# A graph attention layer on one core: three target buffers, scatters behind the queries, strips added four groups back

## What is computed

```python
w_ij = silu(edge_feats @ rad_W1 + rad_b1) @ rad_W2 + rad_b2
w_ij = w_ij + (silu(chi_scalar @ sph_W1 + sph_b1) @ sph_W2 + sph_b2)
q_i = (node_feats @ Wq)[receivers]                 # 8 heads of 16
k_j, v_j = (node_feats @ Wk)[senders], (node_feats @ Wv)[senders]
alpha = (q_i * w_ij * k_j).sum(axis=-1) / sqrt(16) * cutoffs[:, None]
out = segment_sum(alpha[..., None] * v_j, receivers) / 16
return layernorm(node_feats + out)
```

## Time and profile before

| | |
|---|---|
| median of 3 runs | 1971.99 us (1971.89 to 1974.09) |
| the profiled execution | 1972.41 us, of which the program's span 1970.7 us |
| busy share of the span | TensorE matmul 88%, weight load 64%, VectorE 80%, GpSimd 76%, ScalarE 29% |
| granted TensorE clock | 0.937 of 2.4 GHz, mean over the span |
| DMA | 339.02 MB, mean 172 GB/s |

### The profile page before, as it was taken

How to read it: one execution, slowest core, us unless ns; L and a number is a source line. 1 busy time by engine, 2 the same in 40 slices (tenths; PEclk the granted TensorE clock), 3 DMA queues, 4 the chain that set the end, 5 groups by cost and what they waited for, 6 DMA issues and landing times.

```text
span 1970.7 us, 56844 instructions
## 1 busy us (share of the span) xinstructions
PE 1729.7 (88%) x14511; PEld 1261.0 (64%) x14511; DVE 1569.1 (80%) x4324; ACT 580.7 (29%) x1030; POOL 1488.5 (76%) x1569
## 2 busy tenths in 40 slices
PE   8789889898989988888988898989888888898887
PEld 7566666666666656666666666666666666666665
DVE  5578888787877878877978877878778788788787
ACT  5322232222322322322332222232222222222223
POOL 7777777777777777777777777777777777777777
PEclk9899899998988999998999998998899899889898
DMA  9866656666656556556556555656656565656554
GB/s 338 259 172 172 165 163 174 163 169 168 168 161 171 165 166 171 163 165 173 164 164 174 161 167 164 173 164 173 164 165 167 160 175 162 165 163 166 172 156 116
DMA packets 191076, 339.02 MB, mean 172 GB/s; under 512 B 82989, under 2 KB 101022, under 8 KB 190750
## 3 DMA queue, kind: packets, MB, share of 16 engines
q0 software_dynamic: 74240, 202.21, 36.5%
q1 hardware_dynamic: 107440, 126.14, 22.2%
q10 hardware_dynamic: 9070, 7.02, 1.6%
HBM read 320.25 MB, written 14.95 MB: 170 GB/s over the span
## 4 chain that ended last, share of the span: by engine, by line
PE 22%; DMA 21%; SPq 20%; POOL 18%; issue 13%; DVE 5%; DVEq 1%; ACT 0%; ACTq 0%
POOL kvt L655 18%; DMA dbt<-dst 14%; SPq L582 13%; PE bank L693 10%; DMA kvt<-kvtab,srcS 4%; PE bank L670 3%; SPq L576 3%; SPq L591 2%; PE bank L708 2%; DMA out<-partn 2%; PE bank L695 2%; PE bank L732 2%; DVE t L979 1%; PE bank L301 1%; PE bank L683 1%
## 5 line engine op out<-in xcount | busy, mean ns | idle before, releaser
L655 POOL DMA_INDIRECT kvt<-kvtab,srcS x1528 | 1450.9, 950 | 466.3 <-issue 456.5
L770 ACT ACTIVATE hs<-bank,B 128x512 f32<-128x512 f32 x806 | 510.5, 685 | 1350.3 <-issue 804.6
L693 PE MATMUL bank<-W2r,hs 128*128 128x128 f32 x3224 | 499.5, 302 | 8.3 <-ACT hs L770 8.3
L693 PEld LDWEIGHTS bank<-W2r,hs 128*128 128x128 f32 x3224 | 424.2, 205 | 86.6 <-issue 75.3
L693 PE MATMUL bank<-W2s,hs 128*128 128x128 f32 x3224 | 456.7, 288 | 0.0
L966 DVE TENSOR_TENSOR t<-bank,kvt 128x512 f32<-128x512 f32 (+1 forms) x396 | 265.4, 670 | 207.9 <-PE bank L695 131.9
L693 PEld LDWEIGHTS bank<-W2s,hs 128*128 128x128 f32 x3224 | 424.8, 205 | 0.0
L708 PE MATMUL bank<-msg,oh 128*32 128x128 f32 x3216 | 179.0, 294 | 164.0 <-DVE accT L913 160.6
L708 PEld LDWEIGHTS bank<-msg,oh 128*32 128x32 f32 x3216 | 70.6, 110 | 355.7 <-issue 300.4
L981 DVE TENSOR_REDUCE bank<-t 128x32 f32<-128x512 f32 x403 | 280.1, 695 | 13.9
L979 DVE TENSOR_TENSOR t<-bank,t 128x512 f32<-128x512 f32 x403 | 274.2, 680 | 4.2 <-PE bank L683 3.2
(11 more groups left out here) (106 smaller groups left out, 702.7 us busy)
## 6 DMA issues: line engine op xcount, KB each, us to landing
kvA<-kvtab ACTq DMA_DIRECT2D x3968, 1.0 KB
eft<-in_ef SPq DMA_DIRECT2D x102, 512.0 KB, 7.7
kvS<-kvtab SPq DMA_DIRECT2D x3200, 1.0 KB
dbt<-dst SPq DMA_DIRECT2D x102, 384.0 KB, 6.1
kvt<-kvtab,srcS POOLq DMA_INDIRECT x1528
qwt<-qtab SPq DMA_DIRECT2D x403, 24.0 KB
kvtab<-kvt SPq DMA_DIRECT2D x24, 256.0 KB, 7.9
qtab<-qx SPq DMA_DIRECT2D x12, 384.0 KB, 6.3
```

The source lines that it names most:

```text
L655: pool.indirect_dma_start(kvt[:, (g - HX) % KS, t, :], None, kvtab, bass.IndirectOffsetOnAxis(ap=srcS[:, g * TG + t:g * TG + t + 1], axis= ...
L693: pe.matmul(WB[g % 2][:, t * D:(t + 1) * D], hs[:, g % HS, j, t * 128:(t + 1) * 128], w2[:, :], start=(j == 0 and t == 0), stop=False, ski ...
L770: act.activation(hs[:, g % HS, j, :], HB[i % 4][:, :], ACT.Silu, bias=B1[:, j:j + 1]).then_inc(m_si, 1)
```

## The change

- Targets `dbt` get three buffers, and SyncE loads them at g % 4 == 0 instead of g % 4 == 2.
- The first product `t1` gets one buffer instead of two, the messages three instead of four. From group 400 on L999 waits for the scatter of g - 3; in earlier groups `collect(g - 3)` has waited for it.
- TensorE runs in each group: layer 2, the fold of g - 4, the queries, the scatter of g - 3, layer 1. Before, the scatter stood first and the fold was that of g - 3.
- VectorE adds the strips of g - 4 instead of g - 3 and copies those of g - 3 out instead of g - 2. Squares, refinements, scaling and stores of finished nodes come one group later.
- In the prologue the turned features and the remainders lie in two of the three buffers of `eft`, and SyncE waits for the projections of the first groups too.

```diff
-    KS, ES, DS, QS, HS, MS, OS, WS = 15, 3, 2, 6, 4, 4, 3, 6
+    KS, ES, DS, QS, HS, MS, OS, WS = 15, 3, 3, 6, 4, 3, 3, 6
...
-        t1 = sb("t1", [128, 2, TG, D], f32)
+        t1 = sb("t1", [128, TG, D], f32)
...
-            xgT = psb("xgT", [128, 2, G], f32)
+            xgT = eft[:, 2, :, :]
...
-            def qleft(t, b):
-                return t[:, b % 2, 0:min(4, NC - 4 * b), :]
+            qrest = eft[:, 1, :, :].rearrange("p k (a f) -> p k a f", f=D)
+
+            def qleft(b):
+                return qrest[:, b % 2, 0:min(4, NC - 4 * b), :]
...
+            dve.wait_ge(s_win, 4)
             for b in range(NQB + 1):
...
-            act.wait_ge(s_hp, 2 * HX)
+            for eng in (act, sp):
+                eng.wait_ge(s_hp, 2 * HX)
...
-                if b < NQP and (g == 0 or g % 4 == 2 and b >= 2):
+                if g % 4 == 0 and b < NQP:
                     if b >= DS:
                         sp.wait_ge(m_ot, 4 * (b - DS + 1))
...
             for g in range(NE):
-                if 3 <= g < NE - 2:
+                l2(g)
+                if g >= 4:
+                    fold_tiles(g - 4)
+                gq(g)
+                if g >= 3:
                     scat(g - 3)
-                l2(g)
-                if g >= NE - 2:
-                    scat(g - 3)
-                    gq(g)
-                if g >= 3:
-                    fold_tiles(g - 3)
-                if g < NE - 2:
-                    gq(g)
                 if g % 2 == 0 and g // 2 + 1 < NP:
                     l1(g // 2 + 1)
             scat(NE - 3)
+            fold_tiles(NE - 4)
             scat(NE - 2)
...
-                if 3 <= g < NE - 2:
-                    accumulate(g - 3)
+                if 4 <= g < NE - 2:
+                    accumulate(g - 4)
...
-                if 0 <= g - 2 < LC:
-                    collect(g - 2)
+                if 0 <= g - 3 < LC:
+                    collect(g - 3)
                 if g >= NE - 2:
-                    accumulate(g - 3)
+                    accumulate(g - 4)
...
                 dve.wait_ge(m_al, g + 1)
+                if g - MS >= LC:
+                    dve.wait_ge(m_sc, g - MS + 1)
...
+            accumulate(NE - 4)
             accumulate(NE - 3)
             accumulate(NE - 2)
```

More of the change, by code:

```diff
@@ L459, in gnn_program @@
                     act.wait_ge(s_r0, b)
-                    act.activation(qpart(b - 1, 1), qleft(t1, b - 1), ACT.Copy).then_inc(s_q2, 1)
+                    act.activation(qpart(b - 1, 1), qleft(b - 1), ACT.Copy).then_inc(s_q2, 1)
                 if b == NQB // 2:
@@ L475, in gnn_program @@
                         dve.wait_ge(s_q3, b - 1)
-                    dve.tensor_tensor(qleft(t1, b), qfull(b), qpart(b, 0), ALU.subtract).then_inc(s_r0, 1)
+                    dve.tensor_tensor(qleft(b), qfull(b), qpart(b, 0), ALU.subtract).then_inc(s_r0, 1)
                 if b >= 1:
                     dve.wait_ge(s_q2, b)
-                    dve.tensor_tensor(qpart(b - 1, 2), qleft(t1, b - 1), qpart(b - 1, 1),
+                    dve.tensor_tensor(qpart(b - 1, 2), qleft(b - 1), qpart(b - 1, 1),
                                       ALU.subtract).then_inc(s_q3, 1)
@@ L622, in gnn_program @@
                 sp_rows(g)
-                if g - 17 in use_n:
-                    store(use_n[g - 17])
+                if g - 18 in use_n:
+                    store(use_n[g - 18])
             q, b = max(range(0, NQP, ES)), max(range(0, NQP, DS))
@@ L629, in gnn_program @@
             destinations(0, m_db[0])
-            for g in range(NE, NE + 17):
-                if g - 17 in use_n:
-                    store(use_n[g - 17])
+            for g in range(NE, NE + 18):
+                if g - 18 in use_n:
+                    store(use_n[g - 18])
             sp.wait_ge(m_ef[0], features_landed(q) + 16)
@@ L813, in late_collect @@
                     act.activation(part[:, g % 2, :], strips(g)[:, 0:D], ACT.Copy).then_inc(m_part, 1)
-            for g in range(NE + 12):
+            for g in range(NE + 13):
                 if g < NE:
                     silu(g)
[L818 to L821, removed]
+                if g - 6 in use_n and use_n[g - 6] not in late:
+                    square(use_n[g - 6])
+                if g - 13 in use_n and use_n[g - 13] not in late:
+                    scale(use_n[g - 13])
                 if g < NE:
@@ L965, in gnn_program @@
                 for a, b, kv in kv_parts(g):
-                    m = dve.tensor_tensor(t1[:, s, a:b, :], tiles(WB[s][:, :])[:, a:b, :], kv[:, :, 0:D], ALU.mult)
+                    m = dve.tensor_tensor(t1[:, a:b, :], tiles(WB[s][:, :])[:, a:b, :], kv[:, :, 0:D], ALU.mult)
                 m.then_inc(m_t1, 1)
-                if 3 <= g < NE - 2:
-                    accumulate(g - 3)
+                if 4 <= g < NE - 2:
+                    accumulate(g - 4)
                 if g + 2 < NE:
                     window_T(g + 2)
-                if g - 5 in use_n:
-                    first_guess(use_n[g - 5])
+                if g - 6 in use_n:
+                    first_guess(use_n[g - 6])
                 for i in range(3):
-                    if g - 6 - i in use_n:
-                        refine(use_n[g - 6 - i], i)
+                    if g - 7 - i in use_n:
+                        refine(use_n[g - 7 - i], i)
                 dve.wait_ge(m_t1, g + 1)
                 dve.wait_ge(m_q, g + 1)
-                dve.tensor_tensor(t2[:, :, :], tiles(QB[:, :]), t1[:, s, :, :], ALU.mult).then_inc(m_t2, 1)
+                dve.tensor_tensor(t2[:, :, :], tiles(QB[:, :]), t1[:, :, :], ALU.mult).then_inc(m_t2, 1)
                 dve.wait_ge(m_t2, g + 1)
```

## The result

The changed kernel takes 1986.55 us (median of six runs, 1981.92 to 1988.46) against 1973.35 (six runs, 1971.89 to 1974.38) for the kernel before: a ratio of 1.0066 (95% interval 1.0056 to 1.0076; intervals stand in square brackets from here on), 13.2 us slower. The prediction was 1976.0, with a range up to 1982. The profiled execution is the quickest of the six, 1981.92 us, span 1980.2, mean granted clock 0.965 (before 0.937).

A forecast was written before the change was run, and what follows sets the result against it. GpSimd's gathers were taken to set the end, compute having 67 us in hand. Profiled 1972.4 + 0 + 1.3 + 2.7 = 1976.4, less 0.4 for the median: 1976.0 us, range 1973 to 1982.

The forecast's parts named there:

- The price of the path: Loop: product, add, scatter, layer 1, layer 2 now in series; some 0.27 us a group more, between 0 and 0.27.
- the cover: Loop: gathers allow compute 4.685 us a group; 0.09 a group, 37 us, stays in hand, so 0 at the end.
- the 0.19: Loop: VectorE's vanished waits for targets, up to 78.0 us over 403 groups, give back up to 0.19 us a group.
- predicted own pace of 4.59: Loop: compute's time a group without waits for gathers, 4.515 + 0.27 - 0.19 = 4.59 us.
- Step 1 of the tail: Last groups: group 400's rows used at 1951.5 (1951.1 to 1952.3), group 401's first product at 1956.4 (1956.0 to 1957.1).
- step 3: From group 402's first product to the last scatter's end: later adds, scatters and folds in series, +2.7 us (1.5 to 3.0).
- Step 2: Group 401 to 402: scatter 398 waits for a late add ahead of layer 2; 402's first product at 1961.65, +1.3 (0.9 to 2.0).
- the gathers' stream: GpSimd's gathers, untouched: 0 us, +-1; again 1.255 us apart, the last starting within 1 us of 1956.9.
- the 78.0 us of waits for targets worth 0: VectorE's 45 waits for targets go, but the gathers hide the gain: 0 at the end, otherwise up to 78 us.
- the prediction's rival: VectorE bounds the kernel, so removing its target waits takes up to 78.0 us off: 1894 us; chance 0.04.
- the first waits for gathers: Sign on VectorE: its waits for gathered rows begin well before 1200 us and sum to above 67 us.
- outruns the gathers: Loop rival: the new scatter path exceeds 4.685 us a group; 1998 us at 4.75, at most 2011; chance 0.12.

The follow-up runs named there:

- targets alone: Kernel before with only the target buffers and loads, first-product and message buffers and prologue changed, order as before: 1977.00 us, 1.0002 (0.9977 and 0.9978 on slow chips).
- the change again: The changed kernel unaltered, run a second time beside the kernel before for a second profile: 1986.51 us against 1972.85, ratio 1.0070.
- early adds alone: Changed kernel with the adds of the last two groups behind the first product, as in all other groups: 1983.30 us, 1.0031 to the kernel before.
- layer 1 ahead: Changed kernel with layer 1 put ahead of the scatter of g - 3: 1983.24 us, 1.0032 to the kernel before (1.0006 on a slow chip).
- both repairs: Changed kernel with layer 1 before the scatter and the last two groups' adds behind the first product: 1979.69 us, 1.0014 to the kernel before.

## Why the prediction was wrong

**The step that failed** is the one on the loop: "Its cover is the 4.685 that the gathers allow; 0.09 a group, 37 us, is left", costed at 0. The price of the path was right, the cover was not: before the tail's own part begins, group 401's first product is 3.8 us late in the first profile, and 6.0 in the second, counted from its last gather. Three sub-steps:

1. *The mean hid two phases.* From group 7 to 247 compute takes 4.651 us a group before (109.9 to 1226.1) and 4.669 after, though 0.27 was to be added and 0.19 given back; the targets alone take 4.65 too. Some other limit holds that phase, so the 0.19 had nothing to come from. From group 247 to 402, without the waits for gathers, it takes (734.3 - 67.2)/155 = 4.30 before, from 1226.1 to 1960.36, and (737.2 - 27.5)/155 = 4.58 after, from 1229.5 to 1966.73. **The difference is 0.28, the 0.27 of the prediction.** It goes with the order: counted alike, the change again takes 4.62 and the early adds alone 4.56, but the targets alone 4.34, layer 1 ahead 4.36 and both repairs 4.30. That 4.58 is also close to the predicted own pace of 4.59 is luck: the base was 0.21 too high for this phase, and the 0.19 given back never came; over the whole run the prediction's own count gives (1857.7 - 27.5)/395 = 4.63.
2. *What counts is not the margin of the mean but how fast a delay is made good.* By the mean the cover would have done: the gathers come at 4.84 us a group, so 4.58 makes the 22.4 us of group 247 good in some 86 groups of 155, and compute did catch up and wait for rows. But those waits lie ahead of the delays that count at the end. In two quiet stretches, picked from the traces, compute regains 0.89 us a group before (9.21 to 4.75 us late from group 375 to 380), 0.68 in the change (13.89 to 9.14 from 387 to 394). And delays are larger: at groups 369 and 385, each the first product behind a layer 1 with only three gathers, the kernels with layer 1 behind the scatter lose 1.1 to 4.1 us, the others 0.3 to 1.7 (table).
3. *The largest of these delays in the first profile starts at a wait for a gather.* The timeline of the changed kernel at group 384, and its windows (busy us of PE, PEld, DVE, ACT and POOL, granted clock, DMA share, GB/s):

```profile
1881.17 0.69 DVE L967 TENSOR_TENSOR t<-bank,kvt 128x512 f32<-128x512 f32 x1 [1.44 <-DMA kvt<-kvtab,srcS]
...
1882.14 0.66 PE L712 MATMUL bank<-msg,oh 128*32 128x128 f32 x8 [2.42 <-DVE accT L914]
...
1882.73 2.09 PE L674 MATMUL bank<-eft,W 32*128 32x512 f32 x8
...
1884.75 2.08 PE L697 MATMUL bank<-W2r,hs 128*128 128x128 f32 x8
...
1888.81 0.56 DVE L967 TENSOR_TENSOR t<-bank,kvt 128x384 f32<-128x384 f32 x1 [3.37 <-PE bank L699]
```

```profile
1884.00:1887.00 3.00, 3.00 (x14) 2.25 (x11) 1.41 (x5) 1.26 (x2) 2.29 (x3) 0.50 0.37 96
```

VectorE gets its rows late, so its add is late; TensorE, with layer 1 behind the scatter, has nothing to do for 2.42 us; in that wait, at 1881.31, the granted clock falls to 0.50, 1.2 GHz, where it stays until 1888.14; layer 1 and layer 2 take 5.9 us from 1882.73 to 1888.65, where 3.5 would do at 2.4 GHz by the prediction's 1.10 and 2.38; VectorE then waits 3.37 us for TensorE. The wait for a gather, which I had counted as slack, is handed on to the next group as a delay. The Trainium skill ("TensorE: Matmul & The Clock Gate", section on HAM oscillation) describes matmuls that wait inside a loop and start again at the low clock; the 0.50 that begins in the wait of 2.42 us agrees. But low clocks are not more frequent in the change (from 1200 us on the first eight matmuls of layer 2 take over 1.5 us in 10 groups, in 18 before, and the mean granted clock of 1200 to 1950 us is 0.97 against 0.93), so it is the place of the wait and not the clock alone that costs.

That repairing the loop's order restores the catching up is shown (5.5 and 4.9 us late at group 400 with layer 1 ahead, 7.1, 9.2 and 9.2 without). That each of the delays works as at group 384 is read from single places in the traces, not from a removal.

**Step 1 of the tail** was off by this: group 400's rows were to be used at 1951.5, they were used at 1955.13, and 401's at 1959.93 instead of 1956.4. **Step 2** (+1.3) was mis-sized: the mechanism is as told (add 2.1 behind L967, scatter 0.32 behind it), but layer 2 of 402 ran at the low clock, 3.9 us from 1962.73 to 1966.6 instead of 2.38, so 6.80 instead of 5.25: 1.5 us more. I had put the low clock into step 3 and left it out of step 2. **Step 3** (+2.7) measured +3.1, at its upper bound of 3.0.

**What was right**: the gathers' stream (last start 1956.86, predicted within 1 us of 1956.9); the price of the loop's path; TensorE waiting for the add longer than 160.6 (215.9), though in 354 groups and not in every second; and the 78.0 us of waits for targets worth 0 (targets alone: 1.0002). That last one is partly luck. The prediction had the gain hidden by the gathers: compute was to reach its first wait for one sooner. It didn't (1337 us with the targets alone, 1292 before); other waits took the place, and nothing was gained that the gathers could hide. The rule of the Trainium skill ("Perfetto Trace Analysis", section "Identifying the Most-Contended Engine"), to optimize the engine of highest occupancy first, led to VectorE in the prediction's rival; removing these waits of VectorE gave nothing here. **Which sign failed**: the first waits for gathers were to come well before 1200 us and their sum to exceed 67; they came after 1500 and sum to 27.5. That one reading alone tells which step fell. The rival "outruns the gathers" named the right place, but with a threshold of 4.685 that the own pace, 4.63 over the whole run and 4.58 and 4.62 in the last phase, never reached.

Open: which queue or engine holds the first 1200 us; and the 0.14%, some 3 us, that is left with both repairs, of which the profiles show 0.5 us behind the last gather against the kernel before, and 1.4 against the targets alone.

## What to carry to other kernels

A mean over the whole run is no cover where a phase with one limit follows one with another: take the margin from the stretch before the end, as the speed at which a delay is made good there. Independent work (here layer 1) belongs ahead of the instruction that waits, or, as at group 384 here, the wait of one engine becomes the next group's delay on another. A special order for the last iterations has to be gone through again whenever the distance of a dependency changes: the late adds, no cost at a distance of three, cost about as much as the order of the loop at four.

## What the runs showed of the hardware

**Chips differ by half in the time of the same kernel.** On three chips the kernel before takes 3077 to 3107 us, and TensorE's granted clock is 0.77 in the mean. The trace there (targets alone) has stretches in which TensorE, VectorE and here ScalarE stand still and nothing that the profile shows ends them; "remote" stands for a signal whose sender the profile doesn't tell:

```profile
1509.59 0.69 DVE L970 TENSOR_TENSOR t<-bank,kvt 128x512 f32<-128x512 f32 x1 [4.78 <-remote]
...
1511.09 1.27 ACT L774 ACTIVATE hs<-bank,B 128x512 f32<-128x512 f32 x2 [9.71 <-remote]
```

Counted from the records of the seven traces there, 132 to 142 stretches of over 1.5 us with TensorE and VectorE both idle add up to 717 to 794 us; in the kernel before at 1972 us there are 8, 22 us in sum. GpSimd does not stand still with them, as some of the expectations have it: it starts a gather within 121 to 138 of the stretches, in the one shown at 1506.33, 1507.58 and 1508.83. Their cause stays open.

**Gathered rows can be used much later than 3.46 us behind the gather.** The changed kernel's timeline at group 346, whose last gather is the first row:

```profile
1687.29 0.95 POOL L659 DMA_INDIRECT kvt<-kvtab,srcS  x1 [0.30 <-issue]
...
1698.09 0.69 DVE L967 TENSOR_TENSOR t<-bank,kvt 128x512 f32<-128x512 f32 x1 [3.19 <-DMA kvt<-kvtab,srcS]
```

VectorE waits for the rows until 10.8 us behind that gather's start; at the end of the run before it was 3.46. So part of the lateness in the table is landing time and not compute. How large a part is read from the marks that each gather leaves in the trace as it lands, sixteen to a gather. The last mark of a group comes, in the median, 8.5 us behind its last gather's start up to group 247 in the kernel before and 8.9 in the changed one. Of groups 380 to 396 it is 5.1 before, 7.8 and 8.6 in the two profiles of the change and 8.1 with the targets alone. **So up to group 396 much of the table's difference against before is landing, and the kernels with the new buffers and loads share it, whatever their order**; why it is longer there stays open. From group 400 on the rows land within 2.7 to 4.2 us in all kernels of the table. What is left at 401 is compute's: 0.0 us before, 4.4 and 7.5 in the change, 1.7 with the targets alone, 2.8 with layer 1 ahead, 9.1 with the adds early, 2.5 with both.

**One mark in sixteen is the late one.** In those groups of the changed kernel up to 247 whose marks are all in the trace (64), fifteen sixteenths are there 2.9 us behind the last gather's start and the rest at 8.3. With one row load a group moved from SyncE to ScalarE, where the loop runs slower, the landing takes 4.1 us instead of 8.5. Whether the one-row loads cause the late mark was not tested.
